# A Mamba-like layer with an MLP beside it on one TensorE: LoRA's products moved ahead, dt multiplied into the first decay exponential, x itself as values of the state products

## The reference

```python
xn = layernorm(x)                                   # a layer norm ahead of both halves
zxbcdt = xn @ in_proj_w.T                           # z 256, x 256, B and C 64 each, dt 4 heads
dt  = softplus(zxbcdt[..., -4:] + dt_bias)
xBC = silu(causal_conv4(xBC))                       # 4 taps along the sequence
lora  = tanh(xn @ theta_w1) @ theta_w2
theta = clip(theta_base + lora, -pi/2, pi/2)
log_z = complex(-(lambda_base + eta * theta**2) * dt, theta * dt)
x_disc = x_ssm * dt
# scan over chunks: state = exp(cumlog) * state + sum(exp(diff) * B * x_disc); y = Re(C . state)
y = y + x_ssm * D
g = y * silu(z);  g = g * rsqrt(mean(g*g) + eps) * norm_w
out = x + g @ out_proj_w.T + mlp(xn)                # mlp: 128 -> 512 -> 512 -> 128, weights of signs, relu
```

## Time and profile before

| | us |
|---|---|
| median of 3 runs | 353.71 |
| lowest, highest | 353.70, 354.59 |
| the profiled execution | 354.44 |
| its span, first to last instruction | 352.6 |
| PE busy | 297.9 (84%) |
| DVE busy | 282.9 (80%) |
| POOL busy | 181.6 (52%) |
| ACT busy | 172.3 (49%) |

### The profile page before, as it was taken

The page is one execution under the profiler, slowest core; times in us unless marked ns, Lnnn a source line. Parts: engine busy times, 40 slices in busy tenths (PEclk is TensorE's granted clock), DMA queues, the critical chain, the costliest instruction groups (busy, mean ns, idle before and its releaser), DMA issues.

```text
span 352.6 us, 9459 instructions
## 1 busy us (share of the span) xinstructions
PE 297.9 (84%) x3927; PEld 209.6 (59%) x3927; DVE 282.9 (80%) x694; ACT 172.3 (49%) x313; POOL 181.6 (52%) x157
## 2 busy tenths in 40 slices
PE   0467649998999999999999999989998999986690
PEld 0344115677667765776677657775677667753580
DVE  2598898989888988888888898888889887879521
ACT  0404663467545763377437744774467543671110
POOL 0100156205894389718990889168944894194101
PEclk9969586999999999999999999999999999999996
DMA  6400310032002301140113110221013010301001
GB/s 167 104 1 2 92 28 0 3 90 64 6 26 61 90 4 31 41 100 15 33 33 81 42 32 14 73 68 31 2 48 77 0 33 19 95 11 31 2 4 35
DMA packets 19163, 14.85 MB, mean 42 GB/s; under 512 B 5062, under 2 KB 14891, under 8 KB 19115
## 3 DMA queue, kind: packets, MB, share of 16 engines
q1 hardware_dynamic: 16090, 13.67, 15.1%
q10 hardware_dynamic: 3024, 0.52, 0.9%
HBM read 3.70 MB, written 2.10 MB: 16 GB/s over the span
## 4 chain that ended last, share of the span: by engine, by line
DVE 34%; PE 32%; POOL 16%; ACT 8%; issue 6%; DMA 2%; SPq 1%; POOLq 0%; DVEq 0%
POOL btmp L1272 6%; PE bank L1483 5%; POOL btmp L1273 4%; PE bank L1549 4%; PE bank L1564 3%; PE bank L1473 3%; DVE gT L775 3%; PE bank L1431 3%; DVE phl L581 3%; PE bank L1493 3%; DVE cum L613 2%; POOL Ure L1277 2%; POOL Uim L1277 2%; ACT z L1080 2%; POOL rms L1253 2%
## 5 line engine op out<-in xcount | busy, mean ns | idle before, releaser
L1272 POOL TENSOR_TENSOR btmp<-cres,Xre 128x512 f32<-128x512 f32 x8 | 10.7, 1341 | 84.2 <-ACT Xre L1100 84.2
L1464 PE MATMUL bank<-h0h,W 128*128 128x512 f16 x128 | 49.8, 389 | 4.4 <-DVE h1l L784 2.6
L1414 PE MATMUL bank<-XW,xh 128*128 128x256 f16 x256 | 51.6, 289 | 0.0
L1465 PE MATMUL bank<-h0l,W 128*128 128x512 f16 x128 | 49.5, 387 | 0.0
L1414 PE MATMUL bank<-XW,xl 128*128 128x256 f16 x128 | 36.8, 288 | 0.0
L1414 PEld LDWEIGHTS bank<-XW,xh 128*128 128x128 f16 x256 | 26.3, 103 | 8.0 <-issue 0.9
L1132 ACT ACTIVATE h1h<-bank 128x512 f16<-128x512 f32 x32 | 18.1, 589 | 24.9 <-PE bank L1465 24.9
L1464 PEld LDWEIGHTS bank<-h0h,W 128*128 128x128 f16 x128 | 12.8, 100 | 24.0 <-DVE h0l L784 7.2
L784 DVE SCALAR_TENSOR_TENSOR h0l<-bank,h0h 128x512 f16<-128x512 f32 x32 | 21.9, 687 | 6.4 <-ACT h0h L1132 6.2
L784 DVE SCALAR_TENSOR_TENSOR h1l<-bank,h1h 128x512 f16<-128x512 f32 x32 | 22.0, 687 | 5.5 <-ACT h1h L1132 5.2
L1247 POOL TENSOR_TENSOR rstd<-vare,minus_half 128x4 f32<-128x4 f32 x8 | 8.3, 1041 | 34.9 <-DVE negmean L516 34.5
(11 more groups left out here) (211 smaller groups left out, 890.8 us busy)
## 6 DMA issues: line engine op xcount, KB each, us to landing
xtok<-in_x SPq DMA_DIRECT2D x8, 256.0 KB, 3.2
cres<-bc SPq DMA_DIRECT2D x32, 64.0 KB, 2.1
cims<-bc SPq DMA_DIRECT2D x32, 64.0 KB, 2.1
bres<-bc SPq DMA_DIRECT2D x32, 64.0 KB, 2.1
bims<-bc SPq DMA_DIRECT2D x32, 64.0 KB, 2.1
out<-osb SPq DMA_DIRECT2D x8, 256.0 KB, 2.3
const<-constants SPq DMA_DIRECT2D x1, 576.0 KB, 5.6
KT<-in_in_proj_w SPq DMA_DIRECT2D x1, 320.0 KB
```

Source lines behind the costliest of these rows:

```text
L1272: P.tensor_tensor(btmp[0][:], a[:], f1, ALU.mult).then_inc(sig.sem, 1)
L1414: last = M.matmul(dst, tok(x, c, k), w[:, k, :], start=False, stop=(k == TAPS - 1 and q == 2))
L1464: M.matmul(bank[4 + f % 2][:], w, h0h[:, k, :], start=(k == 0), stop=False)
L1465: last = M.matmul(bank[4 + f % 2][:], w, h0l[:, k, :], start=False, stop=(k == MT - 1))
```

## The change

The values of `within` and `new_states` are x itself (`x2s`) in place of `xd`; in their stead the first exponential is multiplied by dt on VectorE (`growth` times `dts`), so that dt enters through K. `dts` is a new copy of the spread dt in SBUF, made by ScalarE (`dt_to_sbuf`); the phase and decay products read it there and no longer in bank 2, so that bank is free earlier for the next `xn_transposed`. The newest tap of the convolution is made by ScalarE (`newest_tap`), and the other three are summed at the end of the turn before. Pairs K, Q, U are each written in one operation of 128x1024 (`decayed`). `largest` runs once at the end.

The order changes too: `lora1` and `bc_products` of n+1 come ahead of `mlp_out(n)`, `lora2` at the head of the turn; `dt_spread` ahead of `g_across`, and `z_products` behind; `xn_transposed` ahead of `out_products`; the sums of squares in two parts; the masks ahead of the phase scan; `states` ahead of the last phase step; both of h0h's last tiles ahead of the first exponential; both of h1l's last tiles ahead of U; the layernorm of n+1 at the head of turn n instead of the end of turn n-1.

The core of the diff (VectorE, ScalarE, TensorE; renamed tiles and the general path, which doesn't run, left out):

```diff
@@ vector
             def bc_taps(n):
                 step = chain(s_conv, n)
-                if not (isinstance(n, int) and n == 0):
-                    v.wait_ge(a_bc.sem, a_bc.at(n, 0))
-                v.wait_ge(t_bc.sem, t_bc.done(n))
-                step(V.tensor_scalar(bcsum[:], bank[2][:], cw[:, 2, PAD:TAPS], None, ALU.mult))
+                v.wait_ge(a_tap.sem, a_tap.done(n))
...
-                v.wait_ge(t_dtr.sem, t_dtr.done(n))
-                step(V.scalar_tensor_tensor(ph[:], theta[:], 1.0 / (2 * math.pi), bank[2][:], ALU.mult, ALU.mult))
+                v.wait_ge(a_dts.sem, a_dts.done(n))
+                step(V.scalar_tensor_tensor(ph[:], theta[:], 1.0 / (2 * math.pi), dts[:], ALU.mult, ALU.mult), linked=False)
+                if ahead_of_scan:
+                    ahead_of_scan()
+                step.link()
...
                 if part == 0:
+                    v.wait_ge(a_exp.sem, a_exp.at(n, 1))
+                    V.tensor_tensor(growth[:], growth[:], dts[:], ALU.mult).then_inc(s_edt.sem, 1)
+                    v.wait_ge(s_edt.sem, s_edt.done(n))
                     v.wait_ge(a_trig.sem, a_trig.done(n))
-                    v.wait_ge(a_exp.sem, a_exp.at(n, 1))
...
-                for dst, src in (((Kre, pcs), (Kim, psn)), ((Qre, Rre[:]), (Qim, Rim[:])), ((Ure, Ure[:]), (Uim, Uim[:])))[part][halves[0]:halves[-1] + 1]:
-                    step(V.tensor_tensor(dst[:], src, growth[:], ALU.mult), linked=False)
+                dst, pitch, src = ((K, 2 * T, X), (Q, T, R), (U, T, U))[part]
+                first, count = halves[0], len(halves)
+                step(V.tensor_tensor(dst[:, first:first + count, :], view(src, 0, 128, pitch * first, [[pitch, count], [1, T]]),
+                                     view(growth, 0, 128, 0, [[0, count], [1, T]]), ALU.mult), linked=False, by=count)
...
@@ vector, pipelined
-                if has_front:
-                    bc_taps(n)
-                if has_back:
-                    for h in EMPTIED:
-                        g_base(n - 1, True, h)
+                if has_next:
+                    early_layernorm(n + 1)
                 if has_front:
                     thetas(n)
-                    phases(n)
-                if has_back:
-                    states(n - 1)
-                if has_front:
+                    phases(n, new_states, masks)
                     exponents(n, True, gates)
...
                 if has_front:
-                    h0_low(n, 1)
                     h0_low(n, 2)
-                    decayed(n, 0, (0,))
                     h0_low(n, 3)
-                    decayed(n, 0, (1,))
+                    decayed(n, 0)
                 if has_next:
                     xn_low(n + 1)
...
-                if has_front:
-                    x_times_dt(n, p)
...
                 if has_front:
                     h1_low(n, 2)
+                    h1_low(n, 3)
                     decayed(n, 2)
-                    h1_low(n, 3)
-                    largest(n)
-                    early_layernorm(n + 2)
+                if has_next:
+                    bc_taps(n + 1)
+                if has_front:
                     add_mlp(n, n % XBUFS)
@@ scalar
+            def newest_tap(n):
+                act.wait_ge(t_bc.sem, t_bc.done(n))
+                step(a_tap, A.activation(bcsum[:], bank[2][:], ACT.Copy, scale=cw[:, 2, PAD:TAPS]))
+
+            def dt_to_sbuf(n):
+                act.wait_ge(t_dtr.sem, t_dtr.done(n))
+                step(a_dts, A.copy(dts[:], bank[2][:]))
@@ tensor
             def lora2(n):
                 pe.wait_ge(a_tanh.sem, a_tanh.done(n))
+                pe.wait_ge(s_conv.sem, s_conv.done(n))
...
             def pipelined(n, p, has_back, has_front, has_next):
                 b = n - 1
                 if has_front:
-                    lora1(n, True)
+                    lora2(n)
...
+                if has_front:
+                    dt_spread(n)
+                if has_back:
                     pe.wait_ge(s_bk.sem, s_bk.done(b))
                     for q in range(2 * NCH):
                         g_across(b, q // 2, q % 2)
                 if has_front:
                     z_products(n)
-                    dt_spread(n)
...
-                if has_front:
-                    mlp1(n, (0, 1))
+                    mlp1(n, (0,))
+                if has_back:
+                    sums_of_squares(b, (2, 3))
+                if has_front:
+                    mlp1(n, (1,))
                     if has_next:
                         dt_products(n + 1)
                         x_products(n + 1, 1)
+                        bc_products(n + 1)
                     mlp1(n, (2, 3))
                     if has_next:
                         x_products(n + 1, 0)
+                        lora1(n + 1, True)
                     mlp_out(n)
-                    if has_next:
-                        bc_products(n + 1)
```

More of the change, by code:

```diff
@@ L606, in exponents @@
                 v.wait_ge(a_nl.sem, a_nl.done(n))
-                step(V.tensor_tensor(lz[:], nl[:], bank[2][:], ALU.mult), linked=False)
+                rates = growth if fast else lz
+                step(V.tensor_tensor(rates[:], nl[:], dts[:], ALU.mult), linked=False)
                 if between:
@@ L611, in exponents @@
                 if fast:
-                    step(V.tensor_tensor_scan(cum3[:, 1, :], all_ones(T), lz[:], 0.0, ALU.mult, ALU.add))
-                    step(V.tensor_scalar(cum3[:, 0, :], cum3[:, 1, :], SAFE, -SAFE, ALU.min, ALU.max), by=2)
+                    step(V.tensor_tensor_scan(growth[:], all_ones(T), growth[:], 0.0, ALU.mult, ALU.add))
+                    step(V.tensor_scalar(cum3[:, 0, :], growth[:], SAFE, -SAFE, ALU.min, ALU.max), by=2)
                 else:
@@ L727, in level_mul @@
                 e = view(E, 0, 128, 0, [[2 * m, nb], [m, 2], [1, m]])
-                for dst, src in ((Wre, Xre), (Wim, Xim)):
-                    V.tensor_tensor(view(dst, 0, 128, 0, [[2 * m, nb], [m, 2], [1, m]]),
-                                    view(src, 0, 128, 0, [[2 * m, nb], [T + m, 2], [1, m]]), e, ALU.mult).then_inc(s_lvmul.sem, 1)
+                for part in range(2):
+                    V.tensor_tensor(view(U, 0, 128, T * part, [[2 * m, nb], [m, 2], [1, m]]),
+                                    view(X, 0, 128, 2 * T * part, [[2 * m, nb], [T + m, 2], [1, m]]), e, ALU.mult).then_inc(s_lvmul.sem, 1)
             def level_take(n, k, m, step):
@@ L1118, in decays @@
                     act.wait_ge(a_exp.sem, a_exp.at(n, 3))
-                    step(a_exp, A.activation(sq[:], sq[:], ACT.Relu, bias=spread[:, 0:1], accum_out=beyond[:]))
+                    step(a_exp, A.activation(sq[:], sq[:], ACT.Relu, bias=spread[:, 0:1], accum_out=beyond[:, n:n + 1]))
                 else:
@@ L1188, in pipelined @@
                 if has_front:
+                    mlp_high(a_h0, t_h0, h0h, n, (2, 3))
                     decays(n, True, 0)
-                    mlp_high(a_h0, t_h0, h0h, n, (2, 3))
                 if has_next:
@@ L1203, in _ @@
             dt_exp(0)
+            newest_tap(0)
+            tanh_lora(0)
             first_turn(0, 0)
@@ L1435, in lora2 @@
                 pe.wait_ge(a_tanh.sem, a_tanh.done(n))
-                for part, into in enumerate((bank[3][:, 0:T // 2], bank[1][:, T // 2:])):
+                pe.wait_ge(s_conv.sem, s_conv.done(n))
+                for part, into in enumerate((bank[3][:, 0:T // 2], bank[2][:, T // 2:])):
                     rows = slice(HALF * part, HALF * part + LORA)
@@ L1489, in g_across @@
             def g_across(n, c, r):
-                k, q = ((Bre, Qre), (Bim, Qim))[r]
+                k = (Bre, Bim)[r]
                 for h in range(HEADS):
@@ L1508, in y_part, with within @@
                 return bank[6 + h // 2][HEAD * (h % 2):HEAD * (h % 2) + HEAD, lo:lo + size]
-            def within(n, c):
+            def within(n, c, values):
                 for h in range(HEADS):
-                    last = M.matmul(y_part(h, CH * c, CH), xd[:, c, HEAD * h:HEAD * h + HEAD], GT[:, h, c, :],
+                    last = M.matmul(y_part(h, CH * c, CH), values[:, c, HEAD * h:HEAD * h + HEAD], GT[:, h, c, :],
                                     start=(c == 0), stop=True, skip_group_check=True)
@@ L1557, in y_wait, with sums_of_squares @@
                 pe.wait_ge(s_g[fast].sem, s_g[fast].done(n))
-                pe.wait_ge(s_xd.sem, s_xd.done(n))
-            def sums_of_squares(n):
+                if not fast:
+                    pe.wait_ge(s_xd.sem, s_xd.done(n))
+            def sums_of_squares(n, chunks):
                 pe.wait_ge(a_gsq.sem, a_gsq.done(n))
-                for c in range(NCH):
+                for c in chunks:
                     for half in range(2):
@@ L1565, in sums_of_squares @@
                                         start=(half == 0), stop=(half == 1))
-                last.then_inc(t_ms.sem, 1)
+                if c == NCH - 1:
```

(7 more changed lines are left out.)

154 lines of the change are left out of this document (82 added, 72 removed).

## The result

The changed kernel takes 359.61 us (median of 4 runs, 358.12 to 361.59) against 353.78 for the kernel before: ratio 1.013, 95% interval 1.008 to 1.018. (The ratio is an estimate of its own over the runs; the quotient of the two medians is 1.016.) It is slower, by more than the 356.0 that I named: I forecast +2.3 us, and it is +4.6 by the ratio and +5.8 by the medians. The median itself lies 0.6 above my high of 359, the ratio put on 353.7 gives 358.3, just inside.

What follows compares the result with a forecast made beforehand. TensorE, busy 35.64 of each 37.27 us turn, was taken as the bound. Turn 0 +1.0, six turns +0.8 (+0.13 each) and turn 7 +0.5 made +2.3 on 353.7: 356.0 us, range 351.5 to 359.

Steps and rivals of the forecast that it cites:

- Rival 1: xl is not late, so the dt products do not wait 0.77; turn 36.63, total 350.9 us, faster; chance 0.21.
- Rival 3: LoRA's first products, ahead of the last MLP layer, wait 0.8 us a turn for U; +5, 361 us; chance 0.09.
- Rival 4: Every table load on the path is followed by idle time as long as itself; 365 us; chance 0.02.
- Rival 2: Gains and losses cancel and turn 0 is absorbed; total 353 to 354.7 us; chance 0.22.
- Last MLP layer to G: bc and LoRA's first products move ahead, leaving add_mlp's time: 2.99 to 2.80 us, -0.19 a turn.
- within to from_state: State copies stand ahead of the last phase step, so TensorE's wait before the products from the states goes: -0.80 a turn.
- dt products to last MLP layer: bc and LoRA's first products come in (0.74 + 0.45), the h1l wait goes (-0.50): +0.69 a turn; U's wait hides.
- from_state to fourth h0 tile: xn transposes stop waiting for the cumulative sum (-0.50, -0.09); half the sums of squares moves behind (0.85): -1.44 a turn.
- Fourth h0 tile to dt products: Dt products wait 0.77 for xl behind h0h, load, exponential, growth times dt and K: 4.18 to 5.80, +1.62 a turn.
- G products to within: dt_spread comes in, LoRA's second products leave, TensorE waits for the last mask: 6.47 to 6.72 us, +0.25 a turn.
- Turn 7: No dt products, but Q, h1l and imaginary products hang on the same exponential, load and K: +0.5 us (0 to 0.8).
- Turn 0: z products behind dt_spread bring mlp0 about 3 us later at half clock, about half absorbed: +1.0 us (0 to 2.5).

Runs made afterwards that it cites:

- dt into K alone: Kernel before with x itself as values, dt copied to SBUF and multiplied into the first exponential, old order and K halves kept: 355.9 us, ratio 1.003.
- xl first: Changed kernel with xl and mean squares ahead of K on VectorE, xh ahead of table load and exponential on ScalarE: 359.02 us, ratio 1.011.
- Masks first: Changed kernel with masks ahead of the phase product, dt_spread behind the z products, silu of z ahead of the dt copy: 355.42 us, ratio 1.003.
- the second profile: The changed kernel run again as it is, beside the other variants: 359.29 us, ratio 1.011 against the kernel before.
- turn 7 filled: Changed kernel with 17 added, unread products in TensorE's idle places of turn 7: 359.61 us, ratio 1.016 against the kernel before.
- both h0h first: Kernel before with only both last h0h tiles moved ahead of the table load and first exponential: 377.85 us, ratio 1.066.
- turn 0 filled: Changed kernel with 19 added, unread products in TensorE's idle places of turn 0: 358.89 us, ratio 1.012 against the kernel before.
- the fastest version: Changed kernel with xl and xh earlier, masks before phase product, turn 0's z products before dt_spread, two h1h tiles before square and excess: 350.95 us, ratio 0.989.

## Why the prediction was right or wrong

The direction and its main reason stand: what the shorter VectorE saved lay off the path, the moves took 2.6 us from three segments of a turn and put 3.0 into the three others. Rivals 1, 3 and 4 fell on single rows: TensorE idles before the dt products; U ends at 256.11 (254.90 + 1.21), ahead of LoRA's first products at 256.82 and with no wait there; the exponential follows the load by 0.01. The Trainium skill adds a drain to every switch of tables ("ScalarE: Activation LUTs", section "What ACT_TABLE_LOAD costs"); the trace disagrees: behind 16 of its 17 loads the next activation starts 0.01 to 0.02 later, and the first, ahead of turn 0, has 1.98 behind it. Rival 2, a cancelling, is what dt into K alone does in the whole (1.003), not this change.

*Last MLP layer to G, within to from_state, dt products to last MLP layer:* forecast to 0.03. GpSimd's second product took 1.26 instead of 2.13 once x times dt was gone, as forecast; with dt into K alone, where little else differs, it took 1.27.

*from_state to fourth h0 tile:* 5.82 for 6.05, 0.23 more gained than forecast. Most of it stands at the out products: from their start to that of what follows it is 1.79 instead of 2.47, where I took off 0.50 for the wait.

*Fourth h0 tile to dt products:* 6.00 for 5.80. Up to the end of xl the chain is within 0.02 of the forecast (5.79 after the tile's start, for 5.77): K took from start to start the 1.14 that I had put. What is missing is a step: the dt products wait for msq too, which takes 0.15 behind xl, and start 0.21 behind the end of xl (244.93 + 0.69) where I had put 0.03. That makes the 0.20. Before xl first ran I took the cure of this wait to be worth 0.7 to 0.9 a turn; the experiment gives 0.4 net.

*G products to within:* **this term was mis-sized:** +0.25 forecast, +0.49 measured. I charged nothing for the phase product ahead of the masks, and at most 0.2 if it were late. It was late: the masks begin 1.41 after the B-K products and not 1.26, for dt_spread, the copy of 0.59 and the product make a chain that ends at 226.5. That is 0.15 of the 0.24; 0.06 more went between G and B-K products and 0.03 behind the masks. Masks first won 0.67 a turn, the 0.15 and the 0.53 of dt_spread.

The turn's miss in all is 0.22 (37.62 for 37.40), 1.3 us in six turns. That it is close to this one term's is luck: the misses of two others, 0.23 less and 0.20 more, cancel.

*Turn 7:* **this term was mis-sized:** +0.5 forecast (0 to 0.8), +1.56 measured, +1.24 in the second profile. I looked at the exponential, load and K, but there VectorE's whole order is late behind them: the third h1 tile waited 2.66 for h1l, where before it waited 1.40. The third tile's row, before and after:

```profile
317.95 0.39 PE L1464 MATMUL bank<-h0h,W 128*128 128x512 f16 x1 [1.40 <-DVE h1l L784]
```

```profile
323.28 0.39 PE L1484 MATMUL bank<-h0h,W 128*128 128x512 f16 x1 [2.66 <-DVE h1l L789]
```

0.95 is the change, 0.6 the half clock, which was in no term (turn 7 filled). Whether the order, the pair operations or K make the 0.95 was not separated; with dt into K alone turn 7 paid 0.73, a stretch at half clock included.

*Turn 0:* +1.0 forecast (0 to 2.5), +2.18 in the profile. But the six profiles with this same turn 0 have the first G products at 68.53 to 71.93, on average 70.4, and two profiles with that of the kernel before (the other is of both h0h first) have them at 69.75 and 69.42. So the term lies between -1.2 and +2.5, and its size hangs on where the half clock falls. That the forecast is near the average is luck: I had it from other steps. With turn 0 filled it is about 0.2 (second G products at 107.50 against 106.94, less 0.36 for turn 1).

*Outside the span:* **not thought of.** Before has 1.7 to 1.9 us there in all its runs, dt into K alone, in the old order, likewise, the changed kernel 2.3 to 3.1. That is about 0.9 of the 5.8 of difference. Of the variants of the changed kernel the three with the masks first have 2.1 to 2.2 in every run and all others 2.2 to 3.4; why stays open.

In sum for the profiled execution, forecast and measured: turn 0 1.0 and 2.2, turns 1 to 6 0.8 and 2.2, turn 7 0.5 and 1.6, end 0 and 0.2, outside 0 and 1.0. In this execution, the longest of the four, the misses all have one sign; in another the 1.2 of turn 0 could as well be missing. The half clock, which moves turn 0 and turn 7, was in no rival.

## What to carry to other kernels

An operation that moves ahead of one on the path must be priced with its own inputs' chain, not with its duration: the phase product cost 0.15 a turn and looked free. An instruction waits for everything that its program says, so read the waits: the 0.15 of msq was in the text of `dt_products`. When arithmetic and order are changed at once, try each part alone: here the arithmetic won 0.35 a turn, the rest lost 0.70, and corrections to the order alone made a kernel 0.8% to 1.1% faster than before. A first and a last turn have other waits than the steady one and want their own segments; here they held 3.7 of 6.2 us in the profile. One profile of such a turn is not enough: the same turn 0 ended 3.4 us apart in six profiles, so compare it with all the kernels that share it before an edit gets the credit.

## What the runs showed of the hardware

Idle places of 1.7 to 3.1 us in an otherwise full TensorE are sometimes followed by some microseconds at 1.2 GHz, half the full clock: behind 3.05 in turn 0, 1.75 in the steady turns of one kernel, 2.66 in turn 7, 1.80 ahead of turn 1's G products. The same wait in the same program doesn't always bring it (a turn of 38.23 beside ones of 41.5; turn 0 with its 3.05 at 1.00 in two profiles of six; turn 7 of the fastest version waits 2.97 at a clock of 1.00). Nor does it need one so long: in turn 7 of dt into K alone the longest idle places ahead of it were 0.80 and 0.54, and the clock from 310 to 312 was 0.50.

Filling turn 7's idle places with products that nobody reads kept the clock at 1.00, where four profiles without them all have a stretch at 0.50. Filling turn 0's shows nothing beyond what happened twice without. The Trainium skill, "TensorE: Matmul & The Clock Gate", section "What's actually happening", says that the gate follows how busy the array was recently; turn 7 filled agrees, as one profile of one place. That its moment differs between runs of one program fits the spread of the variants (352.8 to 358.5 for dt into K alone), but no run here shows why.
